# A fused two-layer kernel on one core: in layer-1 attention, queries and keys projected once and spread through DRAM, probabilities kept whole in fp32, value products on four column groups

## The chip, the core and the metric

The kernel runs on one core of a Trainium2 chip, as one program. The metric is the device time of that program in microseconds (us). The five engines each run their own instruction stream and meet at semaphores: PE (TensorE, matmuls; it loads weights in a second stream, PEld), DVE (VectorE), ACT (ScalarE), POOL (GpSimd) and SP (SyncE, which here only issues DMAs).

## What is computed

There are 32 sequences of 128 tokens, 128 wide, and for each one 77 context tokens. Two layers run, each of gated cross-attention and a gated mixture of experts. The change is in the third line:

```python
x = x + jnp.tanh(g_xattn[0]) * _L0_xattn_ref(_layernorm(x), ctx_1024, ...)          # one head
x = x + jnp.tanh(g_ffn[0])   * _L0_ffn_ref(_layernorm(x), ...)                       # 8 experts, top 2
x = x + jnp.tanh(g_xattn[1]) * _L1_xattn_ref(_layernorm(x), ctx_1024, ctx_1024, ...) # 16 heads of 8
x = x + jnp.tanh(g_ffn[1])   * _L1_ffn_ref(_layernorm(x), ...)                       # 8 experts + shared
# _L1_xattn_ref:
qh = proj(q, wq, bq); kh = proj(k, wk, bk); vh = proj(v, wv, bv)    # each (32, 16, tokens, 8)
scores = jnp.einsum('bhqd,bhkd->bhqk', qh, kh) / math.sqrt(D_K)
scores = jnp.where(mask, jnp.float32(-1000000000.0), scores)
probs = jax.nn.softmax(scores, axis=-1)
out = jnp.einsum('bhqk,bhkd->bhqd', probs, vh)
out = jnp.einsum('bsd,ed->bse', out.transpose(0, 2, 1, 3).reshape(b, -1, D_MODEL), wo) + bo
```

## The kernel before

Four stages follow one another in every engine's program: a (layer-0 attention), b (layer-0 experts), c (layer-1 attention) and d (layer-1 experts). Each treats the 32 sequences, called tiles, as 8 groups of 4 (`TG`). `pipeline` runs a stage in steps; in one step three groups are worked on: `a` is being prepared, `m` is in the middle, `t` is finished. The order inside a step is written by hand for each engine, as a loop over `i` = 0 to 15. That loop and the semaphores set all order.

In stage c, a group has 16 quads: `q` = 4 x tile + `c`, with 4 heads (`j`) in each. The work of a step is this.

- **Preparing group `a`** (`prepare`, `u` = 0 to 7). Queries and keys are kept as high and low parts so that a score can be made in one matmul from them. For that the projected rows stand three times, 32 rows to a head, so the weights are laid out four times as wide: 4 query products of 3 matmuls each (L376 to L378) and 4 key products (L1119). ACT makes the one part (L1244), DVE the other (L1314, L1318). Four matmuls (L1125) make the values. POOL splits them into three bf16 pieces (`c_v3`, L1422 to L1426).
- **Keys into place.** `place_keys` (SP, L1085) moves the keys of one tile into `c_kb`, which is zero elsewhere, by 4 DMAs, 16 for a group; `c_kb` holds two tiles.
- **Scores** (`scores`, L1141 and L1142) for 8 heads (`h` = half a tile, 8 in a group) go to banks 0 and 1. DVE takes the maximum (L1329) and subtracts it (L1335); ACT exponentiates (L1263). The next scores wait for DVE's subtraction, because they use the same banks.
- **Probabilities.** PE turns them (L1154, 4 matmuls for a quad) into bank 2 or 3. ACT copies a high part in fp16 (L1258). The low part is made by DVE for odd quads (L1341), and for even ones by POOL (L1432) from one more copy by ACT (L1257).
- **Value products** (`values`, L1169 and L1170): for each head two matmuls with 30 moving columns, one for each part. DVE adds the three pieces (L1347), inverts the sum (L1352) and divides (L1356).
- **Finishing group `t`.** PE turns the output (`turn_out`, L1177), ACT copies it (L1290), PE projects it (`project`, L1183 and L1186) and DVE adds it to `x_all` (L1362). Then follow layer norm and the router's logits (L286 to L371).

`turn_out` and `project` stand in the same pass `i` = 6, with one group of transposes between them.

## Time and profile before

| | |
|---|---|
| median of 3 runs | 798.11 us (797.28 to 801.21) |
| the profiled execution, its span | 799.2 us (the page gives no other time for it) |
| PE busy | 684.9 us (86%) |
| DVE busy | 632.0 us (79%) |
| ACT busy | 486.1 us (61%) |
| POOL busy | 201.4 us (25%) |
| stage c, from its first scores to the last layer-1 attention residual | 369.5 to 635.1 us of the span |

Busy shares are means over four stages with different limits. PE's busy time counts a matmul from its start to its modelled end, and matmuls overlap, so the distance from one start to the next says more than a duration. One fp32 matmul leaves two records (four value matmuls of L1125 stand as x8); an fp32r matmul and a transpose leave one.

### The profile page before, as it was taken

To read this page: it belongs to the slowest core of one execution; us is meant where nothing else is said; L and a number is where in the kernel's file an instruction comes from. 1 tells how busy PE (TensorE), PEld (TensorE's weight loads), DVE (VectorE), ACT (ScalarE), POOL (GpSimd) and SP (SyncE) were. 2 spreads that over 40 slices of the span, in tenths; PEclk is the share of its full clock that TensorE was granted. 3 is DMA by queue.
4 is the path that set the end of the run, shared out by engine and by line. 5 is a ranking of instruction groups with operands and counts; after the bars stand their busy time and mean duration, and the time that the engine had idled before them with its cause. 6 is when DMAs were issued, how large, how long until landed. Compare 5 with 4: busy or idle time off the path is not lost.

```text
span 799.2 us, 13367 instructions
## 1 busy us (share of the span) xinstructions
PE 684.9 (86%) x4150; PEld 531.9 (67%) x4150; DVE 632.0 (79%) x1325; ACT 486.1 (61%) x769; POOL 201.4 (25%) x255
## 2 busy tenths in 40 slices
PE   5765754999999999977899889899888559999996
PEld 3654542878777877754667667677666348888884
DVE  3666666879888988885989989997998578888886
ACT  3332230777777777754969778786786325555553
POOL 3443230000000000042536637454374200000000
PEclk8777665999999999997989989997998659999999
DMA  5322000000000000001101011010110000000000
GB/s 163 102 97 90 0 0 0 1 1 1 0 0 0 0 0 0 1 8 33 33 18 33 22 28 26 14 38 12 30 24 9 2 1 0 14 13 13 13 27 26
DMA packets 32676, 17.90 MB, mean 22 GB/s; under 512 B 20481, under 2 KB 31490, under 8 KB 32642
## 3 DMA queue, kind: packets, MB, share of 16 engines
q1 hardware_dynamic: 31490, 16.20, 7.6%
q10 hardware_dynamic: 1152, 1.28, 0.6%
q8 instruction: 17, 0.28, 0.1%
q14 instruction: 17, 0.14, 0.1%
HBM read 10.26 MB, written 2.10 MB: 15 GB/s over the span
## 4 chain that ended last, share of the span: by engine, by line
PE 58%; DVE 26%; issue 7%; ACT 4%; POOL 2%; DMA 1%; DVEq 1%; SPq 1%; ACTq 0%; POOLq 0%
PE psum L376 12%; PE psum L378 11%; PE psum L377 11%; DVE c_mx L1329 4%; DVE c_sm L1335 2%; PE psum L1154 2%; DVE c_pl L1341 2%; DVE xn L305 2%; DVE w_hi L1314 2%; PE psum L1186 2%; PE psum L1183 2%; PE psum L864 2%; DVE stats L286 2%; DVE c_on L1356 2%; PE psum L1493 2%
## 5 line engine op out<-in xcount | busy, mean ns | idle before, releaser
L376 PE MATMUL psum<-xh,w_hi 128*128 (+1 forms) x272 | 114.2, 420 | 1.7 <-DVE d_hr L1581 1.7
L377 PE MATMUL psum<-xl,w_hi 128*128 (+1 forms) x272 | 109.7, 403 | 0.0
L378 PE MATMUL psum<-xh,w_lo 128*128 (+1 forms) x272 | 109.4, 402 | 0.0
L1432 POOL TENSOR_TENSOR c_pl<-c_pt,c_ph 77x512 f16<-77x512 f32 x64 | 74.8, 1169 | 123.7 <-ACT c_ph L1258 123.7
L819 DVE TENSOR_TENSOR b_hl<-b_hs,b_hh 128x1024 fp32r<-128x1024 f32 x64 | 78.2, 1221 | 16.8 <-ACT b_hh L813 16.6
L924 ACT ACTIVATE b_hr<-psum,b1s 128x512 f32<-128x512 f32 x128 | 81.0, 685 | 16.4 <-PE psum L378 16.4
L1154 PE MATMUL psum<-ident,c_pf 128*77 128x128 f32 x512 | 86.3, 294 | 4.7 <-DVE c_pl L1341 1.9
L813 ACT ACTIVATE b_hh<-b_hs 128x1024 fp32r<-128x1024 f32 x64 | 68.0, 1062 | 33.4 <-PE psum L378 33.4
L969 DVE TENSOR_TENSOR b_hs<-b_hr,psum 128x1024 f32<-128x1024 f32 x64 | 77.8, 1215 | 12.6 <-ACT b_hr L924 10.8
L1258 ACT ACTIVATE c_ph<-psum 77x512 f16<-77x512 f32 x128 | 74.5, 592 | 6.3 <-PE psum L1154 5.1
L262 POOL TENSOR_TENSOR spare_q<-half_neg 1x1 f32<-1x1 f32 x54 | 10.0, 186 | 221.4 <-DVE mv L289 221.4
L1263 ACT ACTIVATE c_pf<-c_sm,bias_hr,exp_scale 128x616 f32<-128x616 f32 x64 | 57.8, 903 | 12.6 <-DVE c_sm L1335 9.0
L1154 PEld LDWEIGHTS psum<-ident,c_pf 128*77 128x77 f32 x512 | 59.3, 155 | 7.4 <-issue 4.4
L376 PEld LDWEIGHTS psum<-xh,w_hi 128*128 128x128 f32 x272 | 52.7, 194 | 12.7 <-DVE d_hr L1581 2.1
L378 PEld LDWEIGHTS psum<-xh,w_lo 128*128 128x128 f32 x272 | 52.3, 192 | 12.7
L377 PEld LDWEIGHTS psum<-xl,w_hi 128*128 128x128 f32 x272 | 52.8, 194 | 9.8
L1329 DVE TENSOR_REDUCE c_mx<-psum 128x8 f32<-128x616 f32 x64 | 50.6, 791 | 9.7 <-PE psum L1142 9.5
L1543 ACT ACTIVATE d_hr<-psum 128x512 f32<-128x512 f32 x56 | 33.5, 598 | 38.0 <-PE psum L378 38.0
L1335 DVE TENSOR_TENSOR c_sm<-psum,c_mx 128x616 f32<-128x616 f32 x64 | 51.2, 800 | 6.5
L376 PE MATMUL psum<-b_hh,w_hi 128*128 128x512 f32 x128 | 51.0, 398 | 1.0 <-DVE b_hl L819 1.0
L819 DVE TENSOR_TENSOR d_hl<-d_hs,d_hh 128x512 fp32r<-128x512 f32 x56 | 38.7, 692 | 16.0 <-ACT d_hh L813 15.9
L813 ACT ACTIVATE d_hh<-d_hs 128x512 fp32r<-128x512 f32 x56 | 35.4, 633 | 25.2 <-PE psum L378 16.9
(213 smaller groups left out, 1645.3 us busy)
## 6 DMA issues: line engine op xcount, KB each, us to landing
c_kb<-w_lo SPq DMA_DIRECT2D x128, 39.0 KB, 2.0
stage<-in_weights SPq DMA_DIRECT2D x8, 600.0 KB, 4.8
x_all<-in_x SPq DMA_DIRECT2D x8, 256.0 KB, 2.8
out_dram<-x_all SPq DMA_DIRECT2D x8, 256.0 KB, 2.3
ctxg<-in_ctxT SPq DMA_DIRECT2D x8, 156.0 KB, 4.1
ctxg<-in_ctxT ACTq DMA_DIRECT2D x8, 156.0 KB, 2.2
wk<-in_wks SPq DMA_DIRECT2D x1, 256.0 KB
w_wq<-in_wq SPq DMA_DIRECT2D x1, 64.0 KB, 1.8
```

The lines of the kernel that those rows point to most:

```text
L376: pe.matmul(o, wh, h, start=start, stop=False)
L377: pe.matmul(o, wh, l, start=False, stop=False)
L378: return pe.matmul(o, wl, h, start=False, stop=stop)
L813: a_.activation(*self.high(q), ACT.Copy).then_inc(self.hi_done, 1)
L819: v.tensor_tensor(o, i0, i1, ALU.subtract).then_inc(self.lo_done, 1)
L924: ins = a_.activation(Bb["hr"][:, q, c, :], Z[q][c], ACT.Relu, bias=b1s[:, e, c:c + 1])
L969: v.tensor_tensor(Bb["hs"][:, q, :, :], Bb["hr"][:, q, :, :], SBC[q].unsqueeze(1).broadcast_to([P, HC, GT]), ALU.mult).then_inc(xb.scaled, 1)
L1154: ins = pe.transpose(bank[2 + q % 2][0:S2, j * P:(j + 1) * P], pf1[:, h % 2, (q % 2) * HQ + j, :], ident[:])
L1258: a_.activation(ph[:, q % NC4, :], bank[2 + q % 2][0:S2, :], ACT.Copy).then_inc(hi_done, 1)
L1329: v.tensor_reduce(mm, s, AX.X, ALU.max).then_inc(s1_max, 1)
L1335: v.tensor_tensor(sm1[:, h % 2, :, :].rearrange("p (k j) s -> p k j s", k=2), s, mm.unsqueeze(3).broadcast_to([P, 2, HQ, S2]), ALU.subtrac ...
L1432: q_.tensor_tensor(pl_[:, q % NC4, :], pt32[:, q // 2 % 2, :], ph[:, q % NC4, :], ALU.subtract).then_inc(lo_done[0], 1)
```

## The change

It does six things, all in stage c.

1. Queries and keys are projected once, at their natural width: one key matmul and one query product (`NU` = 2 where it was 8). ACT writes the high part and DVE the low part, into `khl` and `qhl`.
2. Both are spread by DMAs through DRAM. SP stores `khl` to `c_k_spread`, waits for it, and reads it back by 12 DMAs into a key tile for the whole group; then the same for the queries, by 3 DMAs. SP also loads the context, which ACT's queue did. The scores of a group wait for all 15 (`qk_in`). Their matmul has 96 rows (`KS`) where it had 128.
3. Probabilities stay in fp32: one copy by ACT for a quad (`copy`), no low parts on DVE or POOL.
4. Value products change sides: the values of a head with a column of ones (77 x 9, fp32) are the weights, and 128 columns of probabilities move. The 4 heads of a quad write to PSUM partitions 0, 32, 64 and 96. `values` runs every second `i`, for two quads.
5. The result lies with heads on partitions, so DVE copies it out (`out_copy`, 128x512) and PE turns it back (`out_back`, 4 transposes for a tile). DVE inverts and divides from there.
6. `turn_out` moves to `i` = 8 and `project` to `i` = 9; the residual is at `i` = 10, where it was at 7, and the layer norm's transposes at 13. POOL keeps only the layer norm.

The core of the diff:

```diff
+        VC = DH + 1
...
-        ph = sb("c_ph", [S2, NC4, HQ * P], F16)
-        pl_ = sb("c_pl", [S2, NC4, HQ * P], F16)
-        pt32 = sb("c_pt32", [S2, 2, HQ * P])
+        pt = sb("c_pt", [S2, NC4, HQ * P])
+        o_t = sb("c_o_t", [P, NC4 * P])
...
+        v4 = sb("c_v4", [S2, 2, TG, NH, VC])
...
+        kb0 = sb("c_kb0", [P, NC4, HQ, TG, SK], F32R)
+        kb1 = w_lo[:, s0:s0 + TG * NC4 * GK].rearrange("p (c j b k) -> p c j b k", c=NC4, j=HQ, b=TG)
+        kb = (kb0[:], kb1)
...
+            def load_context(a):
+                if a.i is None and a.c < 2:
+                    sp.wait_ge(a_v_ready, NG)
+                before(sp, v_ready, 1, a, 0, 2)
+                sp.dma_start(ctxg[:, a.parity, :], ctxT[:, a.cols(GK)]).then_inc(c_ctx[a.parity], 16)
+            def spread_keys(a):
+                p = a.parity
+                before(sp, u_read, NU, a, 0)
+                sp.dma_start(k_dram[p], khl.bitcast(F32)).then_inc(k_spread[p], 16)
+            def place_keys(a):
+                p = a.parity
+                if a.i is None and a.c < 2:
+                    sp.wait_ge(kb_zero, a.c + 1)
+                sp.wait_ge(k_spread[p], a.pair(16, 16))
+                for s, part in enumerate((0, 1, 0)):
+                    for j in range(HQ):
+                        r = 32 * s + DH * j
+                        src = k_dram[p, :, part, :].rearrange("(c j d) k -> j d c k", c=NC4, j=HQ)[j]
+                        sp.dma_start(kb[p][r:r + DH, :, j, :, :].rearrange("d c b k -> d c (b k)").bitcast(F32), src).then_inc(qk_in[p], 16)
+            def spread_queries(a):
+                p = a.parity
+                before(sp, u_read, NU, a, 1)
+                sp.dma_start(q_dram[p], qhl.bitcast(F32)).then_inc(q_spread[p], 16)
+            def place_queries(a):
+                p = a.parity
+                sp.wait_ge(q_spread[p], a.pair(16, 16))
+                if a.i is None and a.c == 0:
+                    sp.wait_ge(xb.used, NG * E)
+                for s, part in enumerate((0, 0, 1)):
+                    src = q_dram[p, :, part, :].rearrange("(c r) t -> r c t", c=NC4)
+                    sp.dma_start(qs[32 * s:32 * s + 32, p, :, :].bitcast(F32), src).then_inc(qk_in[p], 16)
...
+                    load_context(a)
+                    spread_keys(a)
+                    place_keys(a)
+                    spread_queries(a)
+                    place_queries(a)
...
             def prepare(a, u):
-                p = a.parity
                 o = prep_bank(a, u)
                 if u == 0:
                     before(pe, v_copied, 1, a, 0, 1)
-                before(pe, u_read, NU, a, u, 2)
-                if u < NC4:
-                    w = slice(u * P, (u + 1) * P)
-                    ins = product3(pe, o.rearrange("p (a c) -> p a c", a=1), wqh[:, w], wql[:, w],
+                    pe.wait_ge(c_ctx[a.parity], a.pair(16, 16))
+                    ins = pe.matmul(o[:, 0:GK], wk1[:], ctxg[:, a.parity, :], start=True, stop=True)
+                else:
+                    if o is bank[5]:
+                        before(pe, u_read, NU, a, 0)
+                    ins = product3(pe, o.rearrange("p (a c) -> p a c", a=1), wqh, wql,
                                    xh[:, a.cols(1), :], xl[:, a.cols(1), :])
-                else:
-                    if u == NC4:
-                        pe.wait_ge(c_ctx[p], a.pair(16, 16))
-                    c = u - NC4
-                    ins = pe.matmul(o[:, 0:GK], wk1[:, c * P:(c + 1) * P], ctxg[:, p, :], start=True, stop=True)
                 ins.then_inc(u_ready, 1)
...
-                    ins = pe.matmul(o, qs[:, m.parity, c, b * P:(b + 1) * P],
-                                    kb[:, b % 2, c, :, :].rearrange("p j k -> p (j k)"), start=False, stop=True)
+                    ins = pe.matmul(o, qs[0:KS, m.parity, c, b * P:(b + 1) * P],
+                                    kb[m.parity][0:KS, c, :, b, :], start=False, stop=True)
...
-            def values(g, q):
-                b, c = q // NC4, q % NC4
-                before(pe, lo_done[q % 2], NHALF, g, q // 2)
-                if c == 0:
+            def values(g, k):
+                b = k // 2
+                before(pe, pt_done, NQ, g, 2 * k + 1)
+                if k % 2 == 0:
                     before(pe, o_read, TG, g, b, 1)
                     if b == 0:
-                        pe.wait_ge(v_split, g.at(1, 1))
-                for j in range(HQ):
-                    h = c * HQ + j
-                    o = bank[4][:, h * 3 * VW:(h + 1) * 3 * VW]
-                    vv = v3[:, g.parity, b, h, :, :].rearrange("p s d -> p (s d)")
-                    pe.matmul(o, ph[:, q % NC4, j * P:(j + 1) * P], vv, start=True, stop=False)
-                    ins = pe.matmul(o, pl_[:, q % NC4, j * P:(j + 1) * P], vv, start=False, stop=True)
+                        pe.wait_ge(v_copied, g.at(1, 1))
+                        if g.i is None and g.c == 0:
+                            pe.wait_ge(pv_zero, 2)
+                for c in (2 * (k % 2), 2 * (k % 2) + 1):
+                    for j in range(HQ):
+                        ins = pe.matmul(PV[32 * j:32 * j + VC, c * P:(c + 1) * P], v4[:, g.parity, b, c * HQ + j, :],
+                                        pt[:, c, j * P:(j + 1) * P], start=True, stop=True)
                 ins.then_inc(pv_used, 1)
+            def out_back(g, b):
+                before(pe, o_read, TG, g, b)
+                before(pe, o_done, TG, g, b, 1)
+                for c in range(NC4):
+                    ins = pe.transpose(OB[:, c * P:(c + 1) * P], o_t[:, c * P:(c + 1) * P], ident[:])
+                ins.then_inc(ob_ready, 1)
...
-                    g, q = lagged(m, t, i - 6)
-                    if g:
-                        values(g, q)
-                    if t and i == 6:
+                    g, q = lagged(m, t, i - 10)
+                    if g and q % NC4 == 0:
+                        out_back(g, q // NC4)
+                    g, q = lagged(m, t, i - 5)
+                    if g and q % 2 == 1:
+                        values(g, q // 2)
+                    if t and i == 8:
...
-                    if a and m and i < NU:
-                        prepare(a, i)
-                    if t and i == 6:
+                    if a and m and i in (0, 3):
+                        prepare(a, i // 3)
+                    if a and m and i == 6:
+                        prepare_values(a)
+                    if t and i == 9:
...
-                    if a and m and i == NU:
-                        prepare_values(a)
-                    if t and i == 11:
+                    if t and i == 13:
                         ln3.pe_transpose(pe, t)
-                    if t and i == 13:
+                    if t and i == 14:
                         lg1.pe_product(pe, t)
-                    if t and i == 14:
+                    if t and i == 15:
...
+            def copy(g, q):
                 before(a_, t1_ready, NQ, g, q)
-                before(a_, pv_used, NQ, g, q, NC4)
-                if q % 2 == 0:
-                    before(a_, lo_done[0], NHALF, g, q // 2, 2)
-                    a_.activation(pt32[:, q // 2 % 2, :], bank[2][0:S2, :], ACT.Copy)
-                a_.activation(ph[:, q % NC4, :], bank[2 + q % 2][0:S2, :], ACT.Copy).then_inc(hi_done, 1)
+                before(a_, pv_used, NHALF, g, q // 2, 2)
+                a_.activation(pt[:, q % NC4, :], bank[2 + q % 2][0:S2, :], ACT.Copy).then_inc(pt_done, 1)
...
-            def low(g, q):
-                before(v, hi_done, NQ, g, q)
-                before(v, pv_used, NQ, g, q, NC4)
-                v.tensor_tensor(pl_[:, q % NC4, :], bank[2 + q % 2][0:S2, :], ph[:, q % NC4, :],
-                                ALU.subtract).then_inc(lo_done[1], 1)
-            def combine(g, b):
-                before(v, pv_used, NQ, g, NC4 * b + NC4 - 1)
-                v.tensor_reduce(o10[:], bank[4][:, 0:NH * 3 * VW].rearrange("p (h s d) -> p h d s", h=NH, s=3),
-                                AX.X, ALU.add).then_inc(o_read, 1)
+            def out_copy(g, b):
+                before(v, pv_used, NHALF, g, 2 * b + 1)
+                before(v, ob_ready, TG, g, b, 1)
+                v.tensor_copy(o_t[:], PV).then_inc(o_read, 1)
...
-                    go, qo = lagged(m, t, i - 9)
-                    if go and qo % NC4 == 0:
-                        combine(go, qo // NC4)
-                    g, q = lagged(m, t, i - 4)
-                    if g and q % 2 == 1:
-                        low(g, q)
+                    go, qo = lagged(m, t, i - 11)
                     if go and qo % NC4 == 0:
                         invert(go, qo // NC4)
+                    g, q = lagged(m, t, i - 9)
+                    if g and q % NC4 == 0:
+                        out_copy(g, q // NC4)
                     if m and i % 2 == 0:
                         shift(m, i // 2)
-                    if a and m and 0 <= i - 1 < NU:
-                        prepare(a, i - 1)
                     if go and qo % NC4 == 0:
                         divide(go, qo // NC4)
-                    if t and i == 7:
+                    if a and m and i in (2, 5):
+                        prepare(a, i // 3)
+                    if t and i == 10:
```

**PE where `project` stands** (`c_on` is the output, `c_ot` its copy). Before:

```order
L1177 MATMUL psum<-ident,c_on 128x128 x4
L1154 MATMUL psum<-ident,c_pf 77x128 x4
L1071 REGISTER_ALU
L1119 MATMUL psum<-ctxg,wk 128x312
L1181 REGISTER_ALU
L1183 MATMUL psum<-bo_all,ones_row 128x512
L1186 MATMUL psum<-wo,c_ot 128x128 x4
```

After:

```order
L1186 MATMUL psum<-ident,c_on 128x128 x4
L1156 MATMUL psum<-ident,c_pf 77x128 x4
L1059 REGISTER_ALU
L1156 MATMUL psum<-ident,c_pf 77x128 x4
L1059 REGISTER_ALU
L1146 MATMUL psum<-mask_bf,ident_bf 128x312
L1147 MATMUL psum<-w_lo,w_hi 128x312
L1146 MATMUL psum<-mask_bf,ident_bf 128x312
L1147 MATMUL psum<-w_lo,w_hi 128x312
L1190 REGISTER_ALU
L1192 MATMUL psum<-bo_all,ones_row 128x512
L1195 MATMUL psum<-wo,c_ot 128x128 x4
```

The output is now turned two passes after its division, and a pair of score products and a second group of transposes stand between turning and projecting it.

**PE between two score products of a step** (`c_o_t` is DVE's copy of the value products; `c_pt` the probabilities, `c_v` the values). After:

```order
L1147 MATMUL psum<-w_lo,w_hi 128x312
L1059 REGISTER_ALU
L1179 MATMUL psum<-ident,c_o_t 128x128 x4
L1059 REGISTER_ALU
L1171 MATMUL psum<-c_pt,c_v 9x128 x8
L1156 MATMUL psum<-ident,c_pf 77x128 x4
L1059 REGISTER_ALU
```

Eight matmuls of 9 weights columns stand together where each quad had eight of 30 moving columns, and every second time the transposes back stand ahead of them.

**DVE at the start of a step** (`c_oi` is the inverted sum, `c_mx` the maximum). Before:

```order
L1329 TENSOR_REDUCE c_mx<-psum 128x8
L1335 TENSOR_TENSOR c_sm<-psum,c_mx 128x616
L1347 TENSOR_REDUCE c_o<-psum 128x160
L1071 REGISTER_ALU
L1341 TENSOR_TENSOR c_pl<-psum,c_ph 77x512
L1071 REGISTER_ALU
L1352 RECIPROCAL c_oi<-c_o 128x16
L1071 REGISTER_ALU
L1314 SCALAR_TENSOR_TENSOR w_hi<-psum,bq,c_lowpart 128x512
L1356 TENSOR_TENSOR c_on<-c_o,c_oi 128x128
```

After:

```order
L1322 TENSOR_REDUCE c_mx<-psum 128x8
L1328 TENSOR_TENSOR c_sm<-psum,c_mx 128x616
L1334 COPY c_o_t<-psum 128x512
L1059 REGISTER_ALU
L1322 TENSOR_REDUCE c_mx<-psum 128x8
L1328 TENSOR_TENSOR c_sm<-psum,c_mx 128x616
L1059 REGISTER_ALU
L1312 SCALAR_TENSOR_TENSOR w_lo<-psum,bk,w_lo 128x312
L1059 REGISTER_ALU
L1341 RECIPROCAL c_oi<-psum 128x16
L1345 TENSOR_TENSOR c_on<-psum,c_oi 128x128
```

The low parts (L1341 before) are gone, the sum of three pieces has become a plain copy, and the output is divided straight from the bank into which PE turned it.

## Rows read from the trace of the kernel before

**Rows 1.** Windows, inside one step: window and its length, busy, clock, DMA

```profile
448.00:473.00 25.00, 22.22 (x240) 16.92 (x236) 23.71 (x47) 22.11 (x39) 17.18 (x23) 1.00 0.13 29
473.00:480.00 7.00, 6.38 (x30) 4.03 (x31) 3.89 (x7) 2.47 (x4) 0.41 (x1) 0.62 0.07 16
```

**Rows 2.** Timeline of DVE: start us, us, engine, line, operation [idle before]

```profile
396.25 0.80 DVE L1329 TENSOR_REDUCE c_mx<-psum 128x8 f32<-128x616 f32 x1 [0.24 <-PE psum L1142]
...
414.83 0.75 DVE L1362 SCALAR_TENSOR_TENSOR x_all<-psum,tg,x_all 128x512 f32 x1 [2.94 <-PE psum L1186]
...
593.23 0.80 DVE L1329 TENSOR_REDUCE c_mx<-psum 128x8 f32<-128x616 f32 x1 [0.21 <-PE psum L1142]
...
621.79 0.18 DVE L371 COPY logits<-psum 128x32 f32<-128x32 f32 x1
```

**Rows 3.** Timeline of PE at a projection

```profile
475.54 2.07 PE L1183 MATMUL psum<-bo_all,ones_row 1*128 1x512 f32 x2
477.54 2.07 PE L1186 MATMUL psum<-wo,c_ot 128*128 128x128 f32 x8
479.40 0.23 PE L1169 MATMUL psum<-c_v,c_ph 77*128 77x30 bf16 x1
```

**Rows 4.** Groups of DVE, 369:622: count | busy us, mean ns | idle before

```profile
L1341 DVE TENSOR_TENSOR c_pl<-psum,c_ph 77x512 f16<-77x512 f32 x62 | 42.0, 678 | 0.5 <-ACT c_ph L1258 0.4
L1314 DVE SCALAR_TENSOR_TENSOR w_hi<-psum,bq,c_lowpart 128x512 fp32r<-128x512 f32 x28 | 20.3, 726 | 1.3 <-ACT c_lowpart L1244 1.3
L1347 DVE TENSOR_REDUCE c_o<-psum 128x160 f32<-128x480 f32 x30 | 19.4, 648 | 1.2 <-PE psum L1170 1.0
```

**Rows 5.** Timeline of PE inside a step

```profile
447.33 0.69 PE L1119 MATMUL psum<-ctxg,wk 128*128 128x312 f32 x2
447.85 0.18 PE L1169 MATMUL psum<-c_v,c_ph 77*128 77x30 bf16 x1
...
448.06 0.64 PE L1154 MATMUL psum<-ident,c_pf 128*77 128x128 f32 x4
448.54 1.04 PE L1125 MATMUL psum<-wv,ctxg 128*77 128x128 f32 x8
449.41 0.18 PE L1169 MATMUL psum<-c_v,c_ph 77*128 77x30 bf16 x1
...
453.83 0.31 PE L1141 MATMUL psum<-mask_bf,ident_bf 128*128 128x312 bf16 x1 [0.70 <-DVE c_sm L1335]
...
454.40 0.60 PE L324 MATMUL psum<-ident,xn 128*128 128x128 f32 x4
...
456.37 0.31 PE L1141 MATMUL psum<-mask_bf,ident_bf 128*128 128x312 bf16 x1
...
464.94 0.48 PE L376 MATMUL psum<-xh,w_hi 128*128 x1
...
465.73 0.19 PE L1169 MATMUL psum<-c_v,c_ph 77*128 77x30 bf16 x1
```

**Rows 6.** Timeline of PE at the only matmuls with few weight columns

```profile
366.00 0.38 PE L442 MATMUL psum<-wo,bv 128*1 128x128 f32 x2 [1.25 <-DVE exp_scale L433]
366.31 0.38 PE L443 MATMUL psum<-bo,ones_row 1*1 1x128 f32 x2
```

**Rows 7.** Timeline of PE's weight loads, the transposes of Rows 5 at 448.06

```profile
448.04 0.43 PEld L1154 LDWEIGHTS psum<-ident,c_pf 128*77 128x77 f32 x4
```

**Rows 8.** DMA issues: ns of one, min/median/max; then KB, us to landing

```profile
L1085 SPq DMA_DIRECT2D c_kb<-w_lo x128: 585/601/743, 364.9 to 603.5; - x128
...
stage<-in_weights SPq DMA_DIRECT2D x8, 600.0 KB, 4.8
...
out_dram<-x_all SPq DMA_DIRECT2D x8, 256.0 KB, 2.3
```

**Rows 9.** Timeline of DVE, then of PE: from stage b to c

```profile
350.70 0.74 DVE L1314 SCALAR_TENSOR_TENSOR w_hi<-psum,bq,c_lowpart 128x512 fp32r<-128x512 f32 x1
...
369.52 0.42 PE L1141 MATMUL psum<-mask_bf,ident_bf 128*128 128x312 bf16 x1 [2.84 <-DMA c_kb<-w_lo]
```

More of the change, by code:

```diff
@@ L1010, in step @@
             def step(a, m, t):
-                if t and not m:
-                    c_prepare["pool"](q)
                 if t:
                     ln2.pool_rstd(q, t)
-            pipeline(q, step)
+            pipeline(q, step, lambda: c_prepare["pool"](q))
         pool_parts.append(pool_b)
         new_scope()
-        NU = 2 * NC4
+        NU = 2
         NQ = TG * NC4
         NHALF = NQ // 2
-        w1_0, w1_1 = WCOL["w1"][0], WCOL["w2"][1]
-        qs = w_hi[:, w1_0:w1_1].rearrange("p (a c t) -> p a c t", a=2, c=NC4)
@@ L1148, in transpose @@
                 before(pe, s1_exp, NHALF, g, h)
[L1149 to L1152 removed]
+                before(pe, pt_done, NQ, g, q, 2)
                 for j in range(HQ):
@@ L1292, in step @@
                     if g:
-                        high(g, q)
-                    if a and m and i < NU:
-                        prepare(a, i)
-                    if a and m and i == NU:
+                        copy(g, q)
+                    if a and m and i in (1, 4):
+                        prepare(a, i // 3)
+                    if a and m and i == 7:
                         prepare_values(a)
-                    if t and i == 11:
+                    if t and i == 13:
                         ln3.act_high(a_, t)
-                    if t and i == 13:
+                    if t and i == 15:
                         lg1.act_copy(a_, t)
```

213 lines of the change are left out of this document (65 added, 148 removed).

## The prediction

> **What bounds the kernel now.** I read the windows first. In the warm part of a step of stage c, DVE is busy 23.7 of 25.0 us, PE and ACT 22.2 and 22.1, at a granted clock of 1.00, the level of 2.4 GHz [rows 1]. So three engines are nearly full together, and DVE's share is highest. The next 7 us differ: PE's clock is granted at 0.62, a mixture of its two levels, and DVE is busy 3.9 us. DVE's timeline shows why: it waits 2.94 us for the projection before the residual [rows 2], and PE spends 2.00 and 1.86 us on the two parts of it at the lower level [rows 3].
>
> A step is therefore some 26 us of DVE's work and some 7 us of a chain. Steps 1 to 6 run from 396.25 to 593.23, 32.8 us each; step 7 ends with the logits at 621.79, 28.6 us [rows 2]. Only stage c changes noticeably; a, b and d keep their work, except for 4% fewer weight columns to load and split, which I take at nothing.
>
> **What leaves DVE, ACT and POOL.** DVE loses 8 low parts of 0.68 us and 6 of 8 preparations of about 0.7 in a step; the sum of three pieces (0.65) becomes a copy of a like number of elements, for which I take 0.6 to 0.7 [rows 4]. That is 9 to 10 us of 29 to 30, so DVE has about 21 us left. ACT loses 8 copies and 6 preparations, POOL nearly all. Nothing of this is gained as such, since PE comes next.
>
> **PE's work in a step after, warm.** All prices are distances between starts [rows 5].
> - Scores: 8 pairs at 0.57 (453.83 to 454.40) = 4.6 us; for 96 rows instead of 128 I take no saving, as the moving columns stay.
> - Transposes: 16 quads at 0.48 (448.06 to 448.54), 4 new ones back (`out_back`) and 3 for output, layer norm and logits, all at 0.48 = 11.0.
> - Keys 0.52 (447.33 to 447.85), one query product and one router product at 0.79 (464.94 to 465.73), values 0.87 (448.54 to 449.41) = 3.0.
> - Projection: half of 2.00 + 1.86 at the upper level [rows 3] = 1.9.
>
> Together 20.5 us. By the same prices PE's step now has 3 x 0.52 + 3 x 0.79 more, 1.9 less, and 16 value products at 0.21 (447.85 to 448.06): 25.9.
>
> **The value products decide.** A call of `values` now has 8 fp32 matmuls of 128 moving columns, each two records. Records of this form follow each other at 0.109 us (0.87 / 8). No row shows two column groups at work together, so I bound it. One after the other, 16 records take 1.74 us. Wholly side by side in four groups they would take 0.44. I take a value between: the rows of PE start in program order, and the two records of one matmul go to the same group and stand next to each other. So only the second record of one head can run beside the first of the next: 9 record times, 0.98 us. This is a mechanism that I infer, not one that a row shows.
>
> Around each call the array's shape changes twice. The nearest row is the bias product of the setup, the only one with few weight columns: its two records should take 0.21, and the next matmul, in another shape, starts 0.31 after it [rows 6]. That is 0.1 us for a change, 0.2 for a call. A call is then 1.18 us (bounds 0.64 and 1.94), 8 of them 9.4, and PE's step 30.0. I add 0.5 for waits at the layer norm and router, whose chain through POOL and ACT has one pass less: **30.5 us**, PE-bound.
>
> The Trainium skill ("TensorE: Matmul & The Clock Gate", Why this matters for your kernels) gives 2.38 times for three column tiles of 32. An estimate by that figure is 1.74 / 2.38 = 0.73 for the records of a call, and about 770 us for the kernel. No row here shows it.
>
> **The chain of the projection.** After the change two groups of transposes and a pair of scores (1.5 us) stand between `turn_out` and `project`, which covers ACT's copy; the output has been divided a pass earlier. So the 2.94 us wait and the lower clock behind it should go. If that cover fails, about 3 us a step come back, 18 in all. On DVE the residual is queued ahead of the next maximum; DVE has 9 us to spare, so this costs nothing while PE is the bound.
>
> **Keys and queries through DRAM.** SP's chain for a group is: store keys, wait, 12 reads, store queries, wait, 3 reads. Prices [rows 8]: an issue 0.60 us; a landing between 2.3 (256 KB) and 4.8 (600 KB). High: 0.6 + 2.8 + 7.2 + 0.6 + 4.8 + 1.8 + 4.8 = 22.6 us. Low, with issues at two thirds: 0.4 + 2.3 + 4.8 + 0.4 + 2.3 + 1.2 + 2.3 = 13.7. I take 18. It starts about 6 us into a step (at `i` = 2) and is needed at 29. So it is hidden, by 5 us. Behind SP's waits only its own next DMAs are queued.
>
> For group 0 it isn't hidden. It can start about 351, where DVE's first preparation stands [rows 9], and ends at about 369; the first scores now start at 369.52. No change. In step 0 the chain for group 1 starts near 375.5 and ends near 393.5, where the scores of step 1 are now due at about 395.5: 2 us gained. POOL's clearing of the second key tile runs during this.
>
> **Sum.** Steps 1 to 6: 6 x (32.8 - 30.5) = 13.8. Step 7, without preparation: 30.5 - 0.52 - 0.79 - 0.87 = 28.3 against 28.6, 0.3. Step 0: 2. The tail gains a copy and 4 transposes back and loses a low part: -1.5, on the path. Together 14.6 us off the profiled execution's 799.2, which is 1.1 above the median: 784.6, and for the median 783.5. Half a per cent, 4 us, is about what a measurement of this kernel can tell from no change.
>
> **Rivals.**
> - *Full overlap of four groups.* A call is 0.64, PE's step 25.7, with waits 26.5. The score loop (453.83 to 456.37, 2.54 us x 8 = 20.3 [rows 5]) would allow it. 6 x 6.3 + 4.3 + 2 - 1 = 43: 755 us. Against it: the order of records. For it: matmuls of 30 columns start 0.026 apart now, so issue doesn't forbid it. Chance 0.12.
> - *No overlap, slower than before.* PE runs the records of the column groups one after the other. A call is 1.94, a step 20.5 + 15.5 + 0.5 = 36.5: 6 x 3.7 = 22 lost, step 7 34.3, 5.7 lost, tail 3: 829 us. It turns from gain to loss at a call of about 1.47 us, (32.8 - 0.5 - 20.5) / 8. A granted clock that doesn't stay at the upper level through the transposes and narrow matmuls would act alike, and counts here. For it: nothing in the trace shows overlap. Chance 0.30.
> - *The DMA chain is late.* If it takes 28 us where I say 18, every step waits about 5: 810 us or more. Against it: even the high sum is 22.6. Chance 0.05.
> - *Break-even.* A call near 1.47, or a projection that still stalls: 794 to 802. Chance 0.08.
> - *Weight loads that wait.* Four loads of the transposes take 0.43 in all while their matmuls start 0.12 apart [rows 5, 7]: loads run beside matmuls. The Trainium skill ("TensorE: Matmul & The Clock Gate", The mechanism) says loads overlap matmuls in flight only where the row group differs, and here it never does. By that rule, the trace disagreeing for the full array, each record would take its load (0.43 / 4) and its own duration (0.38 - 0.11 [rows 6]) one after the other: 16 x 0.38 = 6.1 us a call, 39 us more a step, above 1,050 us. Chance 0.01.
>
> **How the numbers follow.** My forecast has the remaining 0.44; its own range is a call of 1.0 to 1.4 us, 8 x 7 calls, so -10 and +12: 773 to 796. The range over all cases reaches up to the no-overlap case and leaves out full overlap and little else: 766 to 830. Faster by over 0.5%: 0.12 + 0.42 = 0.54; within: 0.10; slower: 0.36.
>
> **What would show it.** In the new trace: the distance from the first matmul of a `values` call to the transposes behind it (1.2 right, 0.6 or 1.9 for the rivals); starts of its records in pairs, 0.11 apart; steps of 30.5 us with PE waiting under 1 us and the clock near 1.00; no wait of DVE before the residual beyond 0.5 us; the scores of a group never waiting for DMA after step 0. The prediction is wrong if records in different groups don't overlap, if the clock falls inside a step, or if PE waits for ACT's copies, which now stand alone between transposes and values.

## The result and the profile after the change

The changed kernel takes **769.58 us** (median of 4 runs, 768.27 to 771.09) against 797.69 for the kernel before in the same job (4 runs, 797.15 to 801.21): a ratio of **0.9636**, 95% interval 0.961 to 0.9662. That is 28.1 us less. The forecast was 783.5, a gain of 14.6: the sign and the range (766 to 830) held, the size was half of what came.

The profiled execution took 768.41 us with a span of 766.6, so 1.8 us lie around the span. I had set the span of before, 799.2, only 1.1 above the median then shown. With 1.8 around it, it stands some 3 us above the median, so the two traces differ by 32.6 us and the medians by 28. Some 2 of these 3 us may lie in one step of the traced execution of before, 35.6 us long where its likes take 33.3 and 33.7 (windows below). Terms below are compared trace against trace.

Windows over six warm steps of stage c, and the last part of it, in the kernel after (window and its length; then busy us of PE, PEld, DVE, ACT, POOL; clock; DMA share; GB/s):

```profile
396.00:564.00 168.00, 155.79 (x1657) 116.56 (x1655) 122.91 (x255) 109.18 (x179) 20.86 (x30) 1.00 0.30 81
592.00:622.00 30.00, 15.84 (x81) 10.30 (x80) 17.74 (x56) 5.60 (x10) 3.32 (x4) 0.60 0.00 1
```

The same stretch of the kernel before (six steps too):

```profile
396.00:594.00 198.00, 179.40 (x1684) 134.93 (x1682) 175.03 (x344) 154.98 (x267) 105.65 (x139) 0.93 0.11 25
```

DVE was busy 88% of it and is now 73%. PE was 91% and is 93%. The granted clock was 0.93 and is 1.00.

These means hide that the steps of before come in two kinds. Windows from one logits copy to the next, and a residual in a step of the short kind:

```profile
429.53:460.77 31.24, 27.91 (x281) 21.01 (x279) 28.84 (x58) 25.59 (x45) 17.60 (x24) 1.00 0.12 28
460.77:494.43 33.66, 30.77 (x278) 22.76 (x277) 29.10 (x58) 25.51 (x45) 17.46 (x24) 0.90 0.11 24
525.97:561.61 35.64, 32.63 (x280) 24.23 (x279) 29.42 (x58) 25.70 (x45) 17.96 (x24) 0.86 0.12 24
...
446.39 0.75 DVE L1362 SCALAR_TENSOR_TENSOR x_all<-psum,tg,x_all 128x512 f32 x1 [0.86 <-PE psum L1186]
```

In the three long steps the projection ran at the lower level of the clock and the residual waited 2.94 us. In the three short ones it ran at the upper level, at 1.05 us for its first part, and the residual waited 0.86. PE's wait of 1.8 us for DVE's division stood in all six. What [rows 1] to [rows 3] show of the chain of the projection is from the long kind.

DVE's timeline after, the rows that answer to [rows 2] (start us, us, engine, line, operation, idle before it and what ended it):

```profile
370.75 0.80 DVE L1322 TENSOR_REDUCE c_mx<-psum 128x8 f32<-128x616 f32 x1 [2.29 <-PE psum L1147]
...
393.68 0.80 DVE L1322 TENSOR_REDUCE c_mx<-psum 128x8 f32<-128x616 f32 x1 [0.46 <-PE psum L1147]
...
438.25 0.75 DVE L1351 SCALAR_TENSOR_TENSOR x_all<-psum,tg,x_all 128x512 f32 x1 [0.55 <-PE psum L1195]
...
450.19 0.19 DVE L366 COPY logits<-psum 128x32 f32 x1 [3.02 <-PE psum L360]
...
564.03 0.80 DVE L1322 TENSOR_REDUCE c_mx<-psum 128x8 f32<-128x616 f32 x1
...
590.30 0.19 DVE L366 COPY logits<-psum 128x32 f32<-128x32 f32 x1 [2.87 <-PE psum L360]
...
602.36 0.75 DVE L1351 SCALAR_TENSOR_TENSOR x_all<-psum,tg,x_all 128x512 f32<-128x512 f32 x1 [5.51 <-PE psum L1195]
```

Steps 1 to 6 run from 393.68 to 564.03: **28.4 us each** where they took 32.8 [rows 2] and where I had forecast 30.5. The residual waits 0.55 us where it waited 2.94 and 0.86 in turn. A new wait of 3.02 us stands ahead of the logits.

PE's timeline where a step ends, the rows that answer to [rows 5], and a projection, which answers to [rows 3]:

```profile
440.62 0.62 PE L1171 MATMUL psum<-c_pt,c_v 77*9 77x128 f32 x16
441.18 1.13 PE L1156 MATMUL psum<-ident,c_pf 128*77 128x128 f32 x8
442.49 0.31 PE L1146 MATMUL psum<-mask_bf,ident_bf 128*128 128x312 bf16 x1 [0.19 <-DVE c_sm L1328]
...
444.16 0.66 PE L319 MATMUL psum<-ident,xn 128*128 128x128 f32 x4 [0.93 <-POOL xn L312]
...
446.83 0.49 PE L349 MATMUL psum<-xh,w_hi 128*128 x1 [0.42 <-DVE xl L332]
...
449.39 0.66 PE L360 MATMUL psum<-ident,lt_s 128*128 128x128 f32 x4 [0.60 <-ACT lt_s L355]
...
464.78 1.12 PE L1192 MATMUL psum<-bo_all,ones_row 1*128 1x512 f32 x2
465.83 1.16 PE L1195 MATMUL psum<-wo,c_ot 128*128 128x128 f32 x8
466.82 0.60 PE L1179 MATMUL psum<-ident,c_o_t 128*128 128x128 f32 x4
```

A call of `values`, 16 records, takes 441.18 - 440.62 = **0.56 us**. Each record lasts about 0.27, so several are in flight together. That the four column groups are the reason is tested below. The projection takes 466.82 - 464.78 = 2.04 us, against 3.86 at [rows 3]. PE waits at four places of a step. PE's waits, 396 to 564 (line waited for: us in total, times, longest):

```profile
PE psum L319 <- POOL xn L312: 5.6, 6, 0.9
PE psum L360 <- ACT lt_s L355: 3.6, 6, 0.6
PE psum L1146 <- DVE c_sm L1328: 1.7, 8, 0.3
PE psum L349 <- DVE xl L332: 0.9, 3, 0.4
```

These 11.8 us are 1.97 a step.

### The profile page after: what moved, and what is told of

The parts are those of the page before. It is cut to its first block, busy times and chain, and to the rows that moved or that the text cites. A ratio compares the mean times of both kernels' runs of the same rounds, so it can differ in the third digit from the quotient of the medians.

```text
span 766.6 us, 12867 instructions
## 1 busy us (share of the span) xinstructions
PE 656.9 (86%) x4158; PEld 508.3 (66%) x4158; DVE 574.7 (75%) x1211; ACT 427.4 (56%) x657; POOL 92.7 (12%) x121
## 4 chain that ended last, share of the span: by engine, by line
PE 66%; DVE 18%; issue 5%; POOL 5%; ACT 4%; DVEq 1%; DMA 0%; SPq 0%; ACTq 0%; POOLq 0%
PE psum L371 12%; PE psum L373 12%; PE psum L372 12%; PE psum L1156 5%; DVE xn L300 3%; PE psum L1171 3%; DVE stats L281 2%; POOL rstd L293 2%; PE psum L1146 2%; PE psum L360 2%; PE psum L1147 2%; PE psum L1448 2%; PE psum L858 2%; PE psum L349 1%; DVE xl L332 1%
## 5 line engine op out<-in xcount | busy, mean ns | idle before, releaser
L1262 ACT ACTIVATE c_pt<-psum 77x512 f32<-77x512 f32 x128 | 74.9, 586 | 60.5 <-PE psum L1156 60.0
L371 PE MATMUL psum<-xh,w_hi 128*128 (+1 forms) x248 | 102.1, 412 | 2.1 <-DVE d_hr L1536 2.1
L372 PE MATMUL psum<-xl,w_hi 128*128 (+1 forms) x248 | 99.4, 401 | 0.0
L373 PE MATMUL psum<-xh,w_lo 128*128 (+1 forms) x248 | 99.1, 400 | 0.0
L958 DVE TENSOR_TENSOR b_hs<-b_hr,psum 128x1024 f32<-128x1024 f32 x64 | 78.2, 1222 | 12.1 <-ACT b_hr L916 10.9
L1156 PE MATMUL psum<-ident,c_pf 128*77 128x128 f32 x512 | 75.0, 283 | 0.0
L1267 ACT ACTIVATE c_pf<-c_sm,zero_col,exp_scale 128x616 f32<-128x616 f32 x64 | 57.3, 895 | 9.6 <-DVE c_sm L1328 9.6
L319 PE MATMUL psum<-ident,xn 128*128 128x128 f32 x128 | 25.0, 328 | 37.1 <-DVE xn L300 25.0
L372 PEld LDWEIGHTS psum<-xl,w_hi 128*128 128x128 f32 x248 | 47.7, 192 | 9.7
L373 PE MATMUL psum<-b_hh,w_lo 128*128 128x512 f32 x128 | 50.7, 396 | 0.0
L372 PE MATMUL psum<-b_hl,w_hi 128*128 128x512 f32 x128 | 50.4, 394 | 0.0
```

The source lines that it names most:

```text
L371: pe.matmul(o, wh, h, start=start, stop=False)
L372: pe.matmul(o, wh, l, start=False, stop=False)
L373: return pe.matmul(o, wl, h, start=False, stop=stop)
L958: v.tensor_tensor(Bb["hs"][:, q, :, :], Bb["hr"][:, q, :, :], SBC[q].unsqueeze(1).broadcast_to([P, HC, GT]), ALU.mult).then_inc(xb.scaled, 1)
L1156: ins = pe.transpose(bank[2 + q % 2][0:S2, j * P:(j + 1) * P], pf1[:, h % 2, (q % 2) * HQ + j, :], ident[:])
L1262: a_.activation(pt[:, q % NC4, :], bank[2 + q % 2][0:S2, :], ACT.Copy).then_inc(pt_done, 1)
```

## Experiments

Every ratio below is to the kernel before, run on the same chip in the same job. A step is the distance of one logits copy to the next, averaged over five; it is 32.66 us in the kernel before (429.53 to 592.84) and 28.41 in the kernel after.

| run | median us | ratio, 95% interval | `values` call | step |
|---|---|---|---|---|
| the change | 769.58 | 0.9636, 0.961 to 0.9662 | 0.56 | 28.4 |
| e1_one_group | 833.81 | 1.0477, 1.043 to 1.0524 | 1.84 | 36.5 |
| e2_two_groups | 786.03 | 0.9877, 0.983 to 0.9925 | 0.97 | 30.4 |
| e3_group_order | 767.43 | 0.9656, 0.9594 to 0.9717 | 0.58 | 28.5 |
| e4_no_spread | 769.39 | 0.9674, 0.9624 to 0.9724 | | 28.4 |
| e5_project_back | 772.92 | 0.9690, 0.9649 to 0.9731 | | 28.8 |
| e7_dve_work | 779.05 | 0.9760, 0.9719 to 0.9802 | | 29.7 |
| e8_late_clear | 767.34 | 0.9607, 0.9561 to 0.9653 | | 28.4 |
| e10_early_max | 766.97 | 0.9626, 0.9575 to 0.9677 | | 28.1 |
| **e11_reordered** | **757.04** | **0.9507, 0.9462 to 0.9552** | 0.56 | 26.8 |
| e6_before_late | 827.22 | 1.0383, 1.0338 to 1.0427 | | 37 |
| e9_before_project | 798.79 | 1.0014, 0.9984 to 1.0045 | | 32.6 |
| e12_short_low | 772.98 | 0.9682, 0.9634 to 0.9731 | | 28.6 |

### Do the column groups work side by side?

```diff
-  ins = pe.matmul(PV[32 * j:32 * j + VC, c * P:(c + 1) * P], v4[...], pt[...], ...)
+  ins = pe.matmul(PV[0:VC, c * P:(c + 1) * P], v4[...], pt[...], ...)                         # e1
+  ins = pe.matmul(PV[32 * (j % 2):32 * (j % 2) + VC, c * P:(c + 1) * P], v4[...], pt[...], ...)   # e2
```

`PV` is set to 1 instead of 0 at the start of both, so that the unused partitions divide by one.

> The changed kernel, but all four heads of a quad write to the same PSUM partitions 0 to 8, so the value products use one column group (three of four results are overwritten: the attention output is not the reference's; the rest of the work is unchanged). Theory A, the four column groups work side by side and that alone makes a call short: a call of values goes from 0.56 us to 16 x 0.109 + 0.1 = 1.85, PE's step gains 8 x 1.29 = 10.3 us and is PE-bound: step 36 us where it was 28.4, the kernel 820 to 830 us. Theory B, matmuls with 9 weight columns are short by themselves: call 0.56, the kernel 770.

> The changed kernel with the heads of a quad on two column groups, alternating (two of four results are overwritten). Theory A: a call of 8 x 0.109 + 0.1 = 0.97 us, 3.3 us more on PE a step; where PE waits now, part of it is absorbed: step 30 to 31.7, the kernel 781 to 793 us. Theory B (short by themselves): call 0.56, 770 us.

PE's timeline, first of e1, then of e2 (a call, and what follows it):

```profile
446.25 1.92 PE L1171 MATMUL psum<-c_pt,c_v 77*9 77x128 f32 x16
448.09 0.66 PE L1156 MATMUL psum<-ident,c_pf 128*77 128x128 f32 x4
```

```profile
444.78 1.05 PE L1171 MATMUL psum<-c_pt,c_v 77*9 77x128 f32 x16
445.75 1.10 PE L1156 MATMUL psum<-ident,c_pf 128*77 128x128 f32 x8
```

Theory A holds: 1.84, 0.97 and 0.56 us for one, two and four groups. All three lie within 0.02 us of 16 x 0.109 / n + 0.11. So the record price of 0.109 from before's values was right, and n groups divide it by n. The 0.11 us that are left over would be the price of both changes of the array's shape together; no run varied them. In both runs heads also overwrite each other's results, but a record costs no more for it than in before's values, whose four matmuls write to different places.

Run e1 also shows what a full row of PE looks like. Its step is 36.5 us, the figure of my no-overlap rival. It waits only 0.7 of it, so PE's other work is 36.5 - 0.7 - 8 x 1.84 = 21.1 us (my sum: 20.5). The kernel came out at 834, a little above the 820 to 830 I expected.

```diff
-  for c in (2 * (k % 2), 2 * (k % 2) + 1):
-      for j in range(HQ):
+  for j in range(HQ):
+      for c in (2 * (k % 2), 2 * (k % 2) + 1):
```

> The changed kernel with the loops of a call of values exchanged: the two matmuls (four records) of one column group stand next to each other, then the next group. My recorded theory, records start in order and only neighbours of different groups run together: 3 overlaps in 16 records, 13 x 0.109 + 0.1 = 1.5 us a call, 7.5 us more a step, about 810 us. Rival, PE has more than one record of every group in hand and the order hardly matters: call 0.56 to 0.6, 770 us. In between (a group's records wait for each other, but others pass them once started): 1.0 us, 780 to 790.

PE's timeline of e3:

```profile
443.94 0.65 PE L1171 MATMUL psum<-c_pt,c_v 77*9 77x128 f32 x16
444.52 0.66 PE L1156 MATMUL psum<-ident,c_pf 128*77 128x128 f32 x4
```

With four records of one group in a row the call takes 0.58 us, 0.02 more than in alternating order, where the mechanism on which my 1.18 rested asked for 1.5. So it is refuted: groups further down the program are at work while one group still has records in hand. How PE does it no run shows.

### Is the way through DRAM hidden?

```diff
-                    spread_keys(a)
-                    place_keys(a)
-                    spread_queries(a)
-                    place_queries(a)
+                    if a.i is None:        # groups 0 and 1
+                        spread_keys(a)
+                        place_keys(a)
+                        spread_queries(a)
+                        place_queries(a)
-                    pe.wait_ge(qk_in[m.parity], m.pair(240, 240))
+                    if m.i is None and m.c < 2:
+                        pe.wait_ge(qk_in[m.parity], m.pair(240, 240))
```

> The changed kernel, in which groups 2 to 6 leave out the stores of queries and keys to DRAM and the 15 reads (they use what groups 0 and 1 left; their scores are wrong). If the chain is hidden, as I forecast, and its 80 to 110 GB/s disturb nobody: 769 to 771 us. If it costs (scores that wait, or engines slowed by the transfers): each us a step is 5 to 6 us of the kernel, 755 to 765.

(The edit reaches group 7 too, so the chain is left out for groups 2 to 7.)

Windows of e4 in the warm steps, and of the kernel after over the same stretch:

```profile
395.00:560.00 165.00, 153.44 (x1628) 114.79 (x1627) 122.49 (x254) 107.37 (x176) 20.82 (x30) 1.00 0.02 5
```

```profile
395.00:560.00 165.00, 153.61 (x1633) 115.13 (x1631) 122.94 (x254) 107.72 (x176) 20.86 (x30) 1.00 0.31 82
```

The DMA engines' share falls from 0.31 to 0.02, 82 GB/s to 5, and nothing else moves: the step stays at 28.4 us. The chain is hidden, and the transfers slow no engine.

### What is POOL's clearing of keys worth?

```diff
             q_.memset(v4[:, :, :, :, DH:VC], 1.0).then_inc(pv_zero, 1)
+            q_.wait_ge(s1_ready, 1)
             q_.memset(kb[1].bitcast(F32), 0.0).then_inc(kb_zero, 1)
```

> The changed kernel with POOL's clearing of the second key tile (4.3 us) put off until the first scores are made. In the changed kernel it runs beside four DVE operations of the layer norm ahead of stage c, which take 5.05 us where they took 1.11 before. Theory, they share a way to SBUF, and the first scores wait for DVE and not for the DMAs: 3 to 4 us less, 766 us. Rival, the queries' way through DRAM ends last anyway: at most 1 us less.

Timeline ahead of stage c, first of the kernel after, then of e8:

```profile
359.21 5.05 DVE L300 TENSOR_SCALAR xn<-x_all,mv,rstd 128x128 f32<-128x128 f32 x4 [0.84 <-POOL rstd L293]
359.30 4.31 POOL L1398 MEMSET w_lo<- 128x4992 f32 x1
...
369.46 0.44 PE L1146 MATMUL psum<-mask_bf,ident_bf 128*128 128x312 bf16 x1 [0.36 <-ACT bo_all L432]
```

```profile
359.14 1.12 DVE L300 TENSOR_SCALAR xn<-x_all,mv,rstd 128x128 f32<-128x128 f32 x4 [0.84 <-POOL rstd L293]
...
362.11 1.25 SPq L1103 DMA_DIRECT2D w_hi<-c_q_spread  x3
...
367.76 0.42 PE L1146 MATMUL psum<-mask_bf,ident_bf 128*128 128x312 bf16 x1 [3.12 <-issue]
...
369.04 4.26 POOL L1399 MEMSET w_lo<- 128x4992 f32 x1 [9.66 <-PE psum L1147]
```

The contention is real: 5.05 us go back to 1.12. But the first scores start only 1.7 us earlier. The profile names nothing that ended their wait of 3.12 us; the program lets them wait for the reads of keys and queries (issued at 362.11 the last), and the DMA engines go idle at about 367.5, just ahead of them. So the reads now seem to end last. The gain lies between my two expectations, and in the medians 1 to 2 us can't be told from nothing.

### Was the projection's place worth something?

e5 is the kernel after with `project` in the same pass as `turn_out`; e6 and e9 are the kernel before with it moved.

```diff
-                    if t and i == 9:       # e5
+                    if t and i == 8:
                         project(t)
-                    if t and i == 10:
+                    if t and i == 9:
                         residual(t)
-                    if t and i == 6:       # e9 (e6: turn_out 7, project 8, residual and POOL's norm 9, the rest one later)
+                    if t and i == 7:
                         project(t)
-                    if t and i == 7:
+                    if t and i == 8:
                         residual(t)
```

> The changed kernel with project in the same pass as turn_out (i = 8, one group of transposes between them, as before) and the residual one pass earlier (i = 9). Theory, the stall came from that neighbourhood: PE waits about 0.7 us for ACT's copy, DVE 2 to 3 us for the projection, PE's granted clock falls in the steps: 1.5 to 3 us more a step, 780 to 790 us. Rival, DVE and ACT now have enough room that it is absorbed: 769 to 773.

> The kernel before with that part of the change alone: turn_out at i = 7, project at 8, residual at 9, layer norm and router one pass later. In the kernel before, the stall cost up to 1.8 us of PE waiting, 1.9 us of slow projection and 2.9 us of DVE waiting in a step. Theory, it was on the path: 2 to 4 us less a step, 771 to 785 us, so a large part of the measured gain. Rival, DVE is nearly full (28 us of its work in a step of 32.8) and waits elsewhere instead: 793 to 798.

> The kernel before with project alone moved, from i = 6 to 7 (behind a pair of scores), and the residual from 7 to 8; turn_out, layer norm, router and POOL's program stay. In the run with a larger shift, POOL's layer norm stood ahead of its low parts and waited 5.5 us for the statistics, PE's value products waited for POOL 3 us a step. Theory, the same happens here: POOL's norm at i = 8 waits for a later residual, and its low parts behind it reach PE late: 0 to 4 us more a step, 797 to 825 us. Rival, the stall (1.9 us of slow projection, 2.9 of DVE's waiting) goes and nothing takes its place: 775 to 788.

PE's and DVE's timelines of e5:

```profile
437.21 1.12 PE L1192 MATMUL psum<-bo_all,ones_row 1*128 1x512 f32 x2 [0.25 <-ACT c_ot L1289]
438.26 1.16 PE L1195 MATMUL psum<-wo,c_ot 128*128 128x128 f32 x8
439.26 0.60 PE L1156 MATMUL psum<-ident,c_pf 128*77 128x128 f32 x4
...
439.57 0.75 DVE L1351 SCALAR_TENSOR_TENSOR x_all<-psum,tg,x_all 128x512 f32 x1 [1.85 <-PE psum L1195]
```

In the changed kernel DVE does wait 1.85 us again, but the projection keeps the upper level (2.05 us, clock 1.00) and the step grows by 0.4 us only. My theory for e5 asked for a fallen clock and 1.5 to 3 us; the rival was right.

In the kernel before, the same move gains nothing. The window of e9, and its waits of PE, DVE and POOL in it:

```profile
396.00:594.00 198.00, 171.23 (x1680) 130.63 (x1678) 178.36 (x346) 154.44 (x268) 105.69 (x139) 0.97 0.11 25
```

```profile
PE psum L1177 <- DVE c_on L1356: 10.9, 6, 1.8
PE psum L1169 <- POOL c_pl L1432: 7.0, 6, 1.2
...
DVE x_all L1362 <- PE psum L1186: 4.2, 6, 0.9
...
POOL spare_q L262 <- DVE mv L289: 19.7, 6, 4.0
```

The waits ahead of the residual shrink (11.4 us in the kernel before), the clock of that stretch rises from 0.93 to 0.97, and PE waits 7.0 us for POOL instead, whose layer norm (it starts at L262) waits 3.3 us a step for DVE's statistics, where it did not before. The step stays 32.6. With the larger shift of e6 the row of POOL shows the same at full size (its timeline):

```profile
455.33 0.18 POOL L262 TENSOR_TENSOR spare_q<-half_neg 1x1 f32<-1x1 f32 x1 [5.52 <-DVE mv L289]
...
459.70 1.14 POOL L1432 TENSOR_TENSOR c_pl<-c_pt,c_ph 77x512 f16<-77x512 f32 x1
```

The layer norm waits 5.52 us for the statistics, the low parts stand behind it in POOL's row, and PE's value products wait for them. e6 cost 31 us where I had expected a gain of 11 or more: I had moved POOL's norm without asking what was queued behind it. So in the kernel before the move of the projection (point 6 of the change) is not to be had alone: POOL's low parts have to go first.

### What set the step, before and after?

```diff
+                w = HQ * P if g.i is None and g.c == 0 else 8          # e12, on the kernel before
-                v.tensor_tensor(pl_[:, q % NC4, :], bank[2 + q % 2][0:S2, :], ph[:, q % NC4, :], ...)
+                v.tensor_tensor(pl_[:, q % NC4, 0:w], bank[2 + q % 2][0:S2, 0:w], ph[:, q % NC4, 0:w], ...)
+                    if m and i % 2 == 1:                               # e7, on the kernel after
+                        v.tensor_tensor(extra[:], ident[0:S2, :].unsqueeze(1).broadcast_to([S2, HQ, P]),
+                                        ident[0:S2, :].unsqueeze(1).broadcast_to([S2, HQ, P]), ALU.subtract)
```

> The kernel before, in which DVE's low parts of the probabilities (8 in a step, 0.68 us each) cover only the first 8 of 512 columns from group 1 on (the rest stays what group 0 left; the output is not the reference's). Everything else stays, the projection at i = 6 too. This takes about 8 x 0.5 = 4 us of DVE's work from a step and nothing from PE. DVE is busy 29.2 of the 32.8 us of a step, PE's own work is 25.9. Theory, DVE's row of work set the step: 2.5 to 4 us less a step, 770 to 780 us. Rival, PE and the chain of the projection set it: at most 1 us less a step, 790 to 797.

> The changed kernel with one idle DVE operation (77x512 to fp16, from SBUF) in every second pass, 8 in a step, in the places where the low parts of the probabilities stood: about 8 x 0.65 = 5.2 us of DVE's work back. Theory, DVE has that room (busy 20.8 of 28.4 us a step), but the round of scores, maximum and subtraction is in line with it for part of the step: 0 to 2 us more a step, 770 to 784. Rival, the step is set by DVE's round after all: 5 us more a step, 800 or above.

The line of the shortened operation, the window 396 to 564 of e12, and in it PE's wait for DVE's division:

```profile
L1342 DVE TENSOR_TENSOR c_pl<-psum,c_ph x64: 150/152/677, 381.9 to 599.3; 77x8 f16<-77x8 f32 x58, 77x512 f16<-77x512 f32 x6
```

```profile
396.00:564.00 168.00, 156.90 (x1622) 122.44 (x1618) 144.84 (x335) 148.92 (x258) 100.79 (x134) 1.00 0.13 29
```

```profile
PE psum L1177 <- DVE c_on L1357: 2.7, 6, 0.5
```

This is the run that says most about the kernel before. It takes 8 x 0.525 = 4.2 us of DVE's work from a step and nothing else (58 of 64 operations are short, the last two of group 0 among them), and the step falls by 4.1 us, from 32.66 to 28.57. So the step hung on DVE's row of work. The stall of the projection and the low clock were consequences of it: PE waits 2.7 us in six steps for DVE's division where it waited 10.9, and the clock is 1.00 without the projection having moved.

That 4.2 us of work gave 4.1 us does not mean that DVE's work alone filled the step. The short steps of before, with the clock at 1.00 or 0.95, took 31.3 us on average, and all steps of e12 take 28.6. So some 2.8 us of the gain came directly, and the other 1.3 because the long steps with the lower clock are gone.

e12 also sizes up the change. With DVE's low parts cut short, and all else of before in place, the ratio is 0.9682; the whole change, with its 0.9636, is hardly faster. Its output is not the reference's, so it is a measure and no alternative. What each of the other parts of the change is worth by itself (fewer preparations, no low parts on POOL, the new value products) no run shows.

In e7 the added operation takes 0.68 us, on average 0.78 (36.9 us for 47), so 6.3 us of work come to DVE in a step. The step grows by 1.3 us. DVE has room now, but not 6 us of it. The theory (0 to 2 us more a step, 770 to 784) held.

### A version faster than both

e10 moves one thing, e11 four and e8's:

```diff
+                    if a and i == 15:              # DVE, e10 and e11 (and no longer at i == 0)
+                        maximum(a, 0)
+                        shift(a, 0)
                     if t and i == 15:
                         lg1.dve_copy(v, t)
-                    if t and i == 13:              # PE, e11; ACT's high part and DVE's low part one later too
+                    if t and i == 14:
                         ln3.pe_transpose(pe, t)
-                    if t and i == 14:
+                    if t and i == 15:
                         lg1.pe_product(pe, t)
+                    if m and i == 15:              # the next step's i == 0, moved ahead
+                        values(m, 5)
+                        transpose(m, 13)
                     if t and i == 15:
                         lg1.pe_transpose(pe, t)
```

> The changed kernel, with DVE's maximum and subtraction for the next group's first scores ahead of its copy of the logits, where it waits 3.0 us in every step. Theory, PE is what binds (its work is 25.5 to 26 of 28.4 us, it waits 2.4 us in four places, only 0.30 of it for that subtraction): 0.3 us a step, 767 to 769 us. Rival, DVE's 3 us wait is on the path: 1.8 us a step, 12 in all, 757.

> The changed kernel with four moves against PE's waits at the end of a step: the layer norm's transposes from i = 13 to 14, the router's product to 15 behind the next scores, one values call and one group of transposes of the next step's i = 0 put ahead of the logits' transposes, DVE's maximum and subtraction ahead of the logits' copy; and POOL's clearing of the second key tile put off. PE's waits for POOL (0.93), ACT (0.60) and DVE (0.30) go, about 0.5 stays for the low part: 1.9 us a step, 13 in all, and 0 to 2 for the clearing: 754 to 757 us. Rival, the chain of DVE's rounds takes the place of the waits: 762 to 768.

In e10 DVE's wait of 3.0 us ahead of the logits is gone (a wait of 1.67 stands ahead of the maximum instead) and the step shrinks by 0.33 us (its logits run from 419.28 to 559.69 in five steps). That wait, the largest of a warm step in the new trace, was worth one ninth of its size, because PE waited for DVE only 0.30 behind it.

PE's timeline of e11 at a step's end:

```profile
415.86 0.60 PE L319 MATMUL psum<-ident,xn 128*128 128x128 f32 x4
...
418.18 0.49 PE L349 MATMUL psum<-xh,w_hi 128*128 x1 [0.72 <-DVE xl L332]
...
420.12 0.60 PE L360 MATMUL psum<-ident,lt_s 128*128 128x128 f32 x4
```

PE's waits for POOL and ACT are gone, 0.72 us for the low part and 0.19 for a subtraction are left, and the step is 26.8 us. The kernel takes 757.04 us, 5% less than before and 1.3% less than the change (0.9507 against 0.9636; the intervals don't touch). The four moves and the late clearing were not all tried one by one. PE's own work in a step is then 26.8 - 0.9 = 25.9 us, as much as the 25.9 that I had added up for it before the change.

## Why the gain came out twice as large as forecast

**The profile of before** was read rightly as three engines nearly full, DVE first. What I did not do is ask what the step would be if DVE's work alone shrank. I took the 7 us at the lower clock as a chain of its own beside DVE's work. e12 shows it as a consequence of DVE's lateness. I also took the one long step that I had read for all of them, and in half of the six the projection ran at the upper level. The sum did not suffer, as its 32.8 us are the mean of both kinds.

**The value call** is the step that failed: 1.18 us forecast, 0.56 measured, so 8 x 0.62 = 5.0 us a step too much, 30 us in six steps. The bound of 0.64 was right in kind, and even it had the shape change too dear (0.2, by the fit 0.11). I gave the in-order rule, which no row showed and e3 refutes, more weight than the row that spoke against it: matmuls of 30 columns start 0.026 us apart. The Trainium skill ("TensorE: Matmul & The Clock Gate", Why this matters for your kernels), with its 2.38 times for three column tiles, gave an estimate near 770, the measured time, but by two errors that cancel: its call is 0.93 us where 0.56 was measured, and its waits are mine. The runs give 1.84 / 0.97 = 1.9 times for two groups and 1.84 / 0.56 = 3.3 for four, shape changes included. The rival of the weight loads that wait (6.1 us a call) is out by the same 0.56.

**PE's other work** was forecast at 20.5 us and measured 21.1 (e1), and 21.4 by e11's 25.9.

**The waits** were the second error, of the other sign: 0.5 us forecast, 1.97 by the list of waits, and 28.4 - 21.1 - 8 x 0.56 = 2.8 as what is left of the step. The full-overlap rival had nearly the right call (0.64) and made the same error with 0.8 for the waits: its step of 26.5 us and its 755 us are too low for that reason. That my range held the result is therefore in part luck: a call twice too dear and waits far too cheap pull in opposite directions. From my step to the measured one: 30.5 - 5.0 (calls) + 0.6 (other work) + 2.3 (waits) = 28.4.

**The chain of the projection**: the wait of 2.94 us went (0.55 is left) and the clock rose to 1.00, as said. But the distance between turning and projecting was not needed for the clock (e5, in which 1.85 us of the wait are back at a cost of 0.4 a step), and in the kernel before more of it gained nothing (e9).

**DRAM**: right. The first key store is issued at 426.60, the last reads at 436.59; if the scores of group 0 in e8 started when those reads had landed (367.76 - 362.11 = 5.65 behind their issue), the chain ends here at 442.2, and the DMA engines do go idle at about 442: 15.6 us where I took 18, and 5.8 us ahead of the scores at 448.06 where I said 5.

**Group 0**: "no change" came true (370.78 to 370.75), but for another reason than mine. By e8 the DMAs would have allowed 1.7 us less, and POOL's clearing took it.

**The terms**, trace against trace (rows above and [rows 2]): step 0, from first maximum to first maximum, 2.5 us (forecast 2); steps 1 to 6, 26.6 (13.8); step 7 up to the logits 2.3 (0.3); the tail from the logits to the last residual 13.28 to 12.06, 1.2 gained (1.5 lost). Together 32.6, all of the difference of the spans. I had charged the tail with the copy and the transposes back; the low parts that left the same chain seem to have been worth more, which no run tried by itself.

## What to carry to other kernels

Before costing an edit, ask of the trace what the step would be if only the fullest engine lost work: a stall and a fallen clock elsewhere may be its consequence and need no edit of their own. Small fp32 matmuls that write to four different groups of 32 PSUM partitions came at a quarter of their serial time here, in both orders tried, plus 0.11 us a call. After a large change, list the waits of the engine that is now full, not of the one with the largest wait: 1.97 us of PE's waits gave 1.6 us back, DVE's 3.0 us wait gave 0.3.

## What the hardware showed that I had not expected

- Sixteen fp32 records of 9 weight columns and 128 moving columns take 0.56 us on four column groups, 0.97 on two, 1.84 on one, and 0.58 on four with each group's records next to each other. The 16 loads of their weights, all of the same 77 rows, are over in 0.34 us, beside matmuls of 0.27 us each that are in flight: `440.62 0.34 PEld L1171 LDWEIGHTS psum<-c_pt,c_v 77*9 77x9 f32 x16`.
- Four DVE operations from SBUF to SBUF (1.12 us) take 5.05 us beside a POOL memset of 4.31 us; DVE operations that read PSUM (the maximum and the subtraction, 0.80 us each) take the same 0.80 beside it in e8. In e7 one of the eight added SBUF operations of a step takes 1.51 us, beside POOL's layer norm; the others take 0.68. The Trainium skill ("SBUF — State Buffer", SBUF: two separate sides) describes an exclusive lock on ports shared by these two engines, under which the loser waits for the whole instruction; the 5.05 us agree with that.
- Transfers of 82 GB/s beside full engines changed no engine's time: without them the step is 28.4 us as with them (e4).
